# Layer 1 linear attention: quotients in four 32-row strips of the array instead of one 128-row product

## The chip, the cores and the metric

The kernel runs on one core of one Trainium2 chip. The metric is the device time of one execution in microseconds (us), the median over several runs. The engines are named as in the profile: PE is TensorE (PEld its weight loads), DVE is VectorE, ACT is ScalarE, POOL is GpSimd, SP is SyncE. PSUM has eight banks, 0 to 7, of 512 float32 columns.

## The reference, cut to what matters

The whole program is two transformer layers on x[4, 1024, 256]: layer 0 (causal attention plus a mixture of 8 experts, top 2) and layer 1 (linear attention plus an RWKV channel mix). The change is in the attention of layer 1, which has 16 heads of 16 columns:

```python
qkv = (x @ W_qkv).reshape(B, T, 3, H, hd).transpose(2, 0, 3, 1, 4)
q, k, v = (qkv[0], qkv[1], qkv[2])
q = _apply_rope(q, cos, sin)
k = _apply_rope(k, cos, sin)
q_feat = jax.nn.elu(q * SCALE) + 1.0
k_feat = jax.nn.elu(k) + 1.0
kv = jnp.einsum('bhtd,bhtv->bhdv', k_feat, v)
k_sum = k_feat.sum(axis=2)
denom = jnp.maximum(jnp.einsum('bhtd,bhd->bht', q_feat, k_sum), 1e-06)
out = jnp.einsum('bhtd,bhdv->bhtv', q_feat, kv) / denom[..., None]
out = out.transpose(0, 2, 1, 3).reshape(B, T, D)
return out @ W_out
```

Beside it, on the same normed input: `sigmoid(xr @ W_r.T) * (relu(xk @ W_k.T)**2 @ W_v.T)`. Both are added to x.

## The kernel before, in words

`combine_and_layer1` does layer 1 for the four sequences one after the other; `body(b, first, last)` of each engine holds the work of sequence b (0 and 3 written out, 1 and 2 in a loop). There is no scheduler: each engine does its instructions in the order in which they are written, and semaphores join the engines. A sequence is 8 token tiles of 128 tokens, D = 256 columns in DC = 2 chunks `c` of 128, and a chunk holds HP = 8 heads, or NQ = 4 strips of Q = 32 columns with two heads each.

PE's order in a sequence, after the projections q, k, v (L1716 to L1718, from parts), the channel mix's k and r (L1710, L1711) and the transposes of q (L1859):

1. The sums k_feat' v (L1867): per chunk and strip a matmul with 32 columns of weights and 33 moving columns (32 of v and a one, which gives k_sum), into banks 4 and 5. They use four column strips of the array.
2. `mix_values` (L1710, L1711 with act_k): the value product of the channel mix for pairs of token tiles n = 0, 1, 2, in banks 6, 7, 0.
3. `quotients([0, 1])` (L1887): for each token tile i and chunk c one matmul of 128 rows, weights qT (transposed q, kept in xkT, 128 columns), moving `kv` [128, 136]: 128 columns of numerators and 8 of denominators. `kv` is block diagonal over heads, so DVE has masked it (L2274, L2277). One token tile fills one bank, banks 2 to 5 for n = 0, 1.
4. `mix_values([3])` (bank 1), `quotients([2])` (banks 6, 7), `turn_attention(0)` (L1898, transposes of the first four tiles of the result `att` into banks 2, 3), `quotients([3])` (banks 0, 1), `project_out(0)` (L1710, L1711 with wout, banks 4, 5), `turn_attention(1)`, the transposes of the next sequence's first half (L1704), `project_out(1)`, and those of its second half.

All these are float32; the profile has two PE records, each with its weight load, for one such matmul that is not a transpose. So quotients are 16 matmuls and 32 records a sequence.

DVE's order around it: add expert rows for sequence b + 1 (L2103), mask kv (L2274, L2277), more rows (L2103), `scales` (L2134, L2136), `apply_gate(0)` and `(1)` (L2251), `divide(0)` and `(1)`, `apply_gate(2)` and `(3)`, `measure` (L2116, L2120), `divide(2)` and `(3)`, then the sums of the output (L2300). A `divide(n)` serves two token tiles: a maximum (L2258), a reciprocal (L2260) and one multiply per token tile (L2263, [128, 256], from PSUM). A gate reads the bank of a `mix_values` product. ACT copies the transposed q out of banks 0 to 3 (L2065, semaphore qT_ready) and `att` out of banks 2 and 3 (L2074, semaphore oT_ready).

```python
def quotients(pairs):
    for n in pairs:
        if n >= 2:
            pe.wait_ge(gated, NG * b + 2 * (n - 1))
```

Of the kernel before, what the change touches and what calls it, by code (L numbers as in the profile page):

```python
# [1472 lines left out]
def combine_and_layer1(nc, s, expert_out, W_out, mu_r, mu_k, rope_cos, rope_sin, out):  # L1473
# [8 lines left out]
    with ExitStack() as ctx:  # L1482
# [34 lines left out]
        kv = sb("kv", [P, DC, P + HP])  # L1517
        same_head, head_of = sb("same_head", [P, P]), sb("head_of", [P, HP])
# [9 lines left out]
        den = sb("den", [P, 2, 2, DC, HP])  # L1528

# [97 lines left out]
        def _(pool):  # L1627
# [34 lines left out]
            pool.wait_ge(const_ready, 5)  # L1662
            pool.tensor_copy(head_of[:, :], heads[:, :, 0]).then_inc(const_ready, 1)
# [25 lines left out]
        def _(pe):  # L1689
# [126 lines left out]
            def body(b, first, last):  # L1816
# [53 lines left out]
                def mix_values(pairs):  # L1870

                    for n in pairs:
                        if n == 2:
                            pe.wait_ge(qT_ready, 4 * b + 2)
                        for j in range(2):
                            mm = product(ps[:, (6 + n) % 8, j * D:(j + 1) * D],
                                         lambda c: act_k[:, c, tile_of(2 * n + j)], lambda c: wT[:, 2, c, :])
# [3 lines left out]
                def quotients(pairs):  # L1881
                    for n in pairs:
                        if n >= 2:
                            pe.wait_ge(gated, NG * b + 2 * (n - 1))
                        for i in (2 * n, 2 * n + 1):
                            for c in range(DC):
                                mm = pe.matmul(ps[:, (2 + i) % 8, c * (P + HP):(c + 1) * (P + HP)],  # L1887
                                               qT[:, c, tile_of(i)], kv[:, c, :], start=True, stop=True)
                        mm.then_inc(nd_mm, 1)

                def turn_attention(h):
# [4 lines left out]
                    for c in range(DC):  # L1896
                        for i in range(4):
                            mm = pe.transpose(ps[:, 2 + c, tile_of(i)], att[:, 4 * h + i, tile_of(c)], s.ident[:, :])  # L1898
# [16 lines left out]
                quotients([0, 1])  # L1915
                mix_values([3])
                quotients([2])
                turn_attention(0)
                quotients([3])
# [13 lines left out]
        def _(act):  # L1933
# [79 lines left out]
            def body(b, first, last):  # L2013
# [8 lines left out]
                if not first:  # L2022
                    act.wait_ge(nd_mm, NG * b)
# [45 lines left out]
                for m in range(4):  # L2069
# [4 lines left out]
                    act.activation(oT[:, c, h * HB:(h + 1) * HB], ps[:, 2 + c, :], ACT.Copy).then_inc(oT_ready, 1)  # L2074
# [10 lines left out]
        def _(dve):  # L2085
# [117 lines left out]
            def body(b, first, last):  # L2203
# [44 lines left out]
                def apply_gate(n):  # L2248
                    dve.wait_ge(v_mm, NG * b + n + 1)
                    at = gate[:, 2 * n:2 * n + 2, :]  # L2250
                    V.scalar_tensor_tensor(at, at, 1.0, pair_of_tiles(ps[:, (6 + n) % 8, :]), ALU.add, ALU.mult  # L2251
                                           ).then_inc(gated, 1)

                def divide(n):
                    dve.wait_ge(nd_mm, NG * b + n + 1)
                    two = slice((2 + 2 * n) % 8, (2 + 2 * n) % 8 + 2)
# [115 lines left out]
```

## Time and profile before

| | |
|---|---|
| median of 3 runs | 900.39 us (899.24 to 901.1) |
| the profiled execution | 899.21 us |
| its span, first to last instruction | 897.5 us |
| granted TensorE clock, mean | 0.994 of full speed |
| PE busy | 852.9 us, 95% of the span |
| DVE busy | 689.2 us, 77% |
| ACT busy | 523.8 us, 58% |
| POOL busy | 173.2 us, 19% |

Layer 1 is the last quarter of the span; the four places of the change lie near 705 to 717, 761 to 773, 817 to 829 and 873 to 885 us. Matmul records overlap, and a record's length holds its way through the array; the distance from start to start says what one costs PE in a row of them.

### The profile page before, as it was taken

How to read it: one execution, taken by the hardware profiler on the slowest of the kernel's cores; microseconds unless marked ns; L12 is line 12 of the kernel's file. 1: busy time of each engine (PE TensorE's matmuls, PEld its weight loads, DVE VectorE, ACT ScalarE, POOL GpSimd, SP SyncE). 2: the span in 40 equal slices, each digit the busy share in tenths (PEclk: the TensorE clock that was granted, in tenths of full speed). 3: DMA queues.
4: the chain of work that ended last, by engine and by line, in shares of the span. 5: the costliest groups of instructions: out<-in, count | busy, mean ns of one | idle time of the engine just before them, and what ended most of it. 6: DMA issues, size and time to landing. Idle time of an engine off the chain costs nothing. (4 is left out here: it accounts for less than half of the span.)

```text
span 897.5 us, 16848 instructions
## 1 busy us (share of the span) xinstructions
PE 852.9 (95%) x6067; PEld 762.8 (85%) x6067; DVE 689.2 (77%) x1306; ACT 523.8 (58%) x946; POOL 173.2 (19%) x187
## 2 busy tenths in 40 slices
PE   4998989989999999999999999999899999999998
PEld 3787979879999999998989899998787887879877
DVE  6788675566688887888787878785579989899864
ACT  5634354355647565746465665646288678586781
POOL 1000000130120213021111112003506246252202
PEclk9999999999999999999999999999999999999999
DMA  8302000073457575665748383842202122031101
GB/s 288 124 2 95 1 1 1 25 241 121 139 188 259 189 249 184 225 218 196 246 164 279 124 280 128 276 158 60 71 1 65 31 71 72 1 105 35 47 1 48
DMA packets 77396, 112.42 MB, mean 125 GB/s; under 512 B 7552, under 2 KB 64192, under 8 KB 77344
## 3 DMA queue, kind: packets, MB, share of 16 engines
q1 hardware_dynamic: 70864, 94.03, 31.0%
q0 software_dynamic: 6480, 17.70, 6.7%
q8 instruction: 31, 0.51, 0.2%
q14 instruction: 21, 0.17, 0.1%
HBM read 94.02 MB, written 17.69 MB: 124 GB/s over the span
## 5 line engine op out<-in xcount | busy, mean ns | idle before, releaser
L1336 ACT ACTIVATE h<-ps,b1T 128x512 f32<-128x512 f32 (+1 forms) x160 | 90.4, 588 | 126.6 <-PE ps L1200 125.2
L1198 PE MATMUL ps<-w2h,hh 128*128 128x256 f32 x568 | 162.8, 287 | 0.0
L1200 PE MATMUL ps<-w2h,hl 128*128 128x256 f32 x568 | 160.7, 283 | 0.0
L1199 PE MATMUL ps<-w2l,hh 128*128 128x256 f32 x568 | 160.6, 283 | 0.0
L117 POOL DMA_INDIRECT rows<-xn_rows,row_tokens x49 | 49.4, 1007 | 471.1 <-PE ps L1206 310.8
L1441 DVE TENSOR_TENSOR hl<-h,hh 128x512 fp32r<-128x512 f32 x124 | 85.6, 690 | 70.9 <-ACT hh L1340 62.4
L1198 PE MATMUL ps<-xTh,w1h 128*128 128x512 f32 (+1 forms) x320 | 110.6, 345 | 2.4 <-DVE xTl L1383 2.4
L1198 PEld LDWEIGHTS ps<-w2h,hh 128*128 128x128 f32 x568 | 108.6, 191 | 2.4 <-DVE hl L1441 0.2
L1199 PE MATMUL ps<-xTl,w1h 128*128 128x512 f32 (+1 forms) x320 | 110.6, 346 | 0.0
L1199 PEld LDWEIGHTS ps<-w2l,hh 128*128 128x128 f32 x568 | 108.7, 191 | 2.1
L1200 PE MATMUL ps<-xTh,w1l 128*128 128x512 f32 (+1 forms) x320 | 110.0, 344 | 0.0
L1200 PEld LDWEIGHTS ps<-w2h,hl 128*128 128x128 f32 x568 | 108.6, 191 | 0.0
L1340 ACT ACTIVATE hh<-h 128x512 fp32r<-128x512 f32 x124 | 78.4, 633 | 3.9
L127 POOL DMA_INDIRECT raw<-expert_out,slots x48 | 57.8, 1205 | 61.9 <-PE ps L1718 49.5
L1198 PEld LDWEIGHTS ps<-xTh,w1h 128*128 128x128 f32 x320 | 61.4, 192 | 8.0 <-DVE xTl L1383 2.6
L1200 PEld LDWEIGHTS ps<-xTh,w1l 128*128 128x128 f32 x320 | 61.1, 191 | 7.4
L1199 PEld LDWEIGHTS ps<-xTl,w1h 128*128 128x128 f32 x320 | 61.2, 191 | 5.0
L1716 PE MATMUL ps<-wqkvh,xh 128*128 128x256 f32 (+1 forms) x128 | 43.6, 341 | 2.4 <-DVE folded L2093 2.4
L1717 PE MATMUL ps<-wqkvl,xh 128*128 128x256 f32 (+1 forms) x128 | 43.3, 338 | 0.0
L1377 DVE TENSOR_TENSOR w2l<-raw,w2h 128x512 fp32r<-128x512 f32 x60 | 41.6, 694 | 2.1
L1718 PE MATMUL ps<-wqkvh,folded 128*128 128x256 f32 (+1 forms) x128 | 43.1, 337 | 0.0
L611 ACT ACTIVATE shared<-ps,neg_max 128x1024 f32<-128x1024 f32 (+7 forms) x24 | 17.6, 737 | 42.6 <-DVE neg_max L916 42.6
(327 smaller groups left out, 2173.4 us busy)
## 6 DMA issues: line engine op xcount, KB each, us to landing
raw<-in_L_ffn_W SPq DMA_DIRECT2D x30, 1024.0 KB, 5.0
raw_odd<-in_L_ffn_W SPq DMA_DIRECT2D x28, 1024.0 KB
expert_out<-y SPq DMA_DIRECT2D x11, 512.0 KB
shared<-in_L_ffn_b SPq DMA_DIRECT2D x9, 512.0 KB
b2row<-in_L_ffn_b SPq DMA_DIRECT2D x29, 128.0 KB, 8.7
x_acc<-in_L_attn_x SPq DMA_DIRECT2D x3, 1024.0 KB, 8.8
xn_rows<-raw SPq DMA_DIRECT2D x3, 1024.0 KB, 4.4
out<-x_acc SPq DMA_DIRECT2D x3, 1024.0 KB
```

Of the source, the lines that this page charges most:

```text
L117: pool.indirect_dma_start(out=rows_part(s, tile, part), out_offset=None, in_=xn_rows, in_offset=bass.IndirectOffsetOnAxis(ap=token, axis=0 ...
L127: pool.indirect_dma_start(out=s.picked_rows[:, i, k, :], out_offset=None, in_=expert_out, in_offset=bass.IndirectOffsetOnAxis(ap=slot, axi ...
L1198: pe.matmul(out, ah, bh, start=start, stop=False, skip_group_check=True)
L1199: pe.matmul(out, ah, bl, start=False, stop=False, skip_group_check=True)
L1200: return pe.matmul(out, al, bh, start=False, stop=stop, skip_group_check=True)
L1336: op = act.activation(h32[:, at, cols], ps[:, slot, cols], ACT.Relu, bias=s.b1T[:, ds(e * HC + w * tile.chunks + n, 1)])
L1340: act.activation(hh[:, slot, 0:tile.width], h32[:, at, 0:tile.width], ACT.Copy).then_inc(h_hi, 1)
L1377: V.tensor_tensor(w2l[:, u, ks], w2raw[u][:, ks], w2h[:, u, ks].bitcast(F32), ALU.subtract).then_inc(w2_lo, 1)
L1441: V.tensor_tensor(hl[:, slot, at], h32[:, slot % 2, at], hh[:, slot, at].bitcast(F32), ALU.subtract).then_inc(h_lo, 1)
L1716: pe.matmul(dst, ah(c), bh(c), start=(c == 0), stop=False)
L1717: pe.matmul(dst, ah(c), bl(c), start=False, stop=False)
L1718: mm = pe.matmul(dst, al(c), bh(c), start=False, stop=(c == DC - 1))
```

## The change

The quotients are computed per strip: for each token tile, chunk and strip q of 32 rows, one matmul whose weights are 32 rows and 128 columns of qT and whose moving tensor is 34 columns of `kv` (32 numerators, 2 denominators). `kv` becomes [128, 2, 34]; the mask is 32 columns wide (`same_in_strip`, reduced once from `same_head` on DVE before the sequences; a POOL copy falls away). Strip q writes to bank 4 + q for token tiles 0 to 3 and to bank q for tiles 4 to 7. So there are 64 matmuls a sequence instead of 16, in two calls of 32, each with one semaphore increment at its end; `divide` reads four banks and multiplies in four instructions instead of two. The value products move to banks 0 to 3, and each waits for ACT's copy of the transposed q out of that bank. `turn_attention(0)` writes to banks 6 and 7. Before the second call PE waits for all four gates.

```diff
@@ -1514,8 +1514,9 @@
         Q, NQ = 32, P // 32
         v1 = sb("v1", [P, BT, DC, NQ, Q + 1])
         qT = xkT
-        kv = sb("kv", [P, DC, P + HP])
-        same_head, head_of = sb("same_head", [P, P]), sb("head_of", [P, HP])
+        HQ = Q // HD
+        kv = sb("kv", [P, DC, Q + HQ])
+        same_head, same_in_strip = sb("same_head", [P, P]), sb("same_in_strip", [P, Q])
...
+        def quotient_columns(i, c, q):
+
+            at = ((i % 4) * DC + c) * (Q + HQ)
+            return ps[:, 4 * (1 - i // 4) + q, at:at + Q + HQ]
+
+        def quotients_of(n):
+
+            first = 4 * (1 - n // 2)
+            at = n % 2 * 2 * DC * (Q + HQ)
+            return ps[:, first:first + NQ, at:at + 2 * DC * (Q + HQ)].rearrange("p q (m f) -> p m q f", f=Q + HQ)
+
+        def turned_bank(h, c):
+
+            return (6 if h == 0 else 2) + c
...
                     for n in pairs:
-                        if n == 2:
-                            pe.wait_ge(qT_ready, 4 * b + 2)
+                        pe.wait_ge(qT_ready, 4 * b + n + 1)
                         for j in range(2):
-                            mm = product(ps[:, (6 + n) % 8, j * D:(j + 1) * D],
+                            mm = product(ps[:, n, j * D:(j + 1) * D],
                                          lambda c: act_k[:, c, tile_of(2 * n + j)], lambda c: wT[:, 2, c, :])
                         mm.then_inc(v_mm, 1)
...
-                def quotients(pairs):
-                    for n in pairs:
-                        if n >= 2:
-                            pe.wait_ge(gated, NG * b + 2 * (n - 1))
-                        for i in (2 * n, 2 * n + 1):
-                            for c in range(DC):
-                                mm = pe.matmul(ps[:, (2 + i) % 8, c * (P + HP):(c + 1) * (P + HP)],
-                                               qT[:, c, tile_of(i)], kv[:, c, :], start=True, stop=True)
-                        mm.then_inc(nd_mm, 1)
+                def quotients(half):
+                    if half:
+                        pe.wait_ge(gated, NG * b + NG)
+                    for i in range(4 * half, 4 * half + 4):
+                        for c in range(DC):
+                            for q in range(NQ):
+                                of = slice(q * Q, (q + 1) * Q)
+                                mm = pe.matmul(quotient_columns(i, c, q), qT[of, c, tile_of(i)], kv[of, c, :],
+                                               start=True, stop=True)
+                    mm.then_inc(nd_mm, 1)
...
-                            mm = pe.transpose(ps[:, 2 + c, tile_of(i)], att[:, 4 * h + i, tile_of(c)], s.ident[:, :])
+                            mm = pe.transpose(ps[:, turned_bank(h, c), tile_of(i)], att[:, 4 * h + i, tile_of(c)],
+                                              s.ident[:, :])
...
-                quotients([0, 1])
+                quotients(0)
                 mix_values([3])
-                quotients([2])
                 turn_attention(0)
-                quotients([3])
+                quotients(1)
                 project_out(0)
...
                 def divide(n):
-                    dve.wait_ge(nd_mm, NG * b + n + 1)
-                    two = slice((2 + 2 * n) % 8, (2 + 2 * n) % 8 + 2)
-                    nd = ps[:, two, 0:DC * (P + HP)].rearrange("p j (c f) -> p j c f", c=DC)
-                    V.tensor_scalar(den[:, n % 2], nd[:, :, :, P:P + HP], 1e-6, None, ALU.max).then_inc(den_step, 1)
+                    dve.wait_ge(nd_mm, 2 * b + n // 2 + 1)
+                    nd = quotients_of(n)
+                    V.tensor_scalar(den[:, n % 2].rearrange("p j c (q h) -> p (j c) q h", h=HQ), nd[:, :, :, Q:Q + HQ], 1e-6, None,
+                                    ALU.max).then_inc(den_step, 1)
...
                     for j in range(2):
-                        op = V.tensor_tensor(att[:, 2 * n + j, :].rearrange("p (c h f) -> p c h f", c=DC, f=HD),
-                                             nd[:, j, :, 0:P].rearrange("p c (h f) -> p c h f", f=HD),
-                                             den[:, n % 2, j].unsqueeze(3).to_broadcast([P, DC, HP, HD]), ALU.mult)
+                        for c in range(DC):
+                            at = slice(c * P, (c + 1) * P)
+                            op = V.tensor_tensor(att[:, 2 * n + j, at].rearrange("p (q h f) -> p q h f", q=NQ, f=HD),
+                                                 nd[:, j * DC + c, :, 0:Q].rearrange("p q (h f) -> p q h f", f=HD),
+                                                 den[:, n % 2, j, c].rearrange("p (q h) -> p q h", h=HQ).unsqueeze(3)
+                                                 .to_broadcast([P, NQ, HQ, HD]), ALU.mult)
                     op.then_inc(att_ready, 1)
...
-                for c in range(DC):
-                    V.tensor_tensor(kv[:, c, 0:P].rearrange("p (q f) -> p q f", f=Q),
-                                    ps[:, 4 + c, 0:Q].unsqueeze(1).to_broadcast([P, NQ, Q]),
-                                    same_head[:, :].rearrange("p (q f) -> p q f", f=Q), ALU.mult)
-                    op = V.tensor_scalar(kv[:, c, P:P + HP], head_of[:, :], ps[:, 4 + c, Q:Q + 1], None, ALU.mult)
-                op.then_inc(kv_ready, 1)
+                V.tensor_tensor(kv[:, :, 0:Q], ps[:, 4:4 + DC, 0:Q],
+                                same_in_strip[:, :].unsqueeze(1).to_broadcast([P, DC, Q]), ALU.mult)
+                V.tensor_tensor(kv[:, :, Q:], ps[:, 4:4 + DC, Q:Q + 1].to_broadcast([P, DC, HQ]),
+                                same_in_strip[:, 0:Q:HD].unsqueeze(1).to_broadcast([P, DC, HQ]), ALU.mult
+                                ).then_inc(kv_ready, 1)
```

PE, the loop body of sequences 1 and 2, from the third value product on (`wT,act_k` is `mix_values`, `kv,xkT` the quotients, `ident,att` the transposes of the result, `wout,oT` the output product). Before:

```order
L1710 MATMUL ps<-wT,act_k 128x256 [waits qT_ready]
L1711 MATMUL ps<-wT,act_k 128x256
L1710 MATMUL ps<-wT,act_k 128x256
L1711 MATMUL ps<-wT,act_k 128x256
L1887 MATMUL ps<-kv,xkT 128x136 [waits kv_ready,qT_ready]
L1887 MATMUL ps<-kv,xkT 128x136 x7
L1710 MATMUL ps<-wT,act_k 128x256
L1711 MATMUL ps<-wT,act_k 128x256
L1710 MATMUL ps<-wT,act_k 128x256
L1711 MATMUL ps<-wT,act_k 128x256
L1887 MATMUL ps<-kv,xkT 128x136 [waits gated]
L1887 MATMUL ps<-kv,xkT 128x136 x3
```

Behind these rows stand, before the change, `turn_attention(0)` (8 transposes, waits att_ready), then 4 more quotients (wait gated), then the output product. Now:

```order
L1901 MATMUL ps<-kv,xkT 128x34 [waits kv_ready,qT_ready]
L1901 MATMUL ps<-kv,xkT 128x34 x31
L1724 MATMUL ps<-wT,act_k 128x256 [waits qT_ready]
L1725 MATMUL ps<-wT,act_k 128x256
L1724 MATMUL ps<-wT,act_k 128x256
L1725 MATMUL ps<-wT,act_k 128x256
L1912 MATMUL ps<-ident,att 128x128 [waits att_ready]
L1912 MATMUL ps<-ident,att 128x128 x7
L1901 MATMUL ps<-kv,xkT 128x34 [waits gated]
L1901 MATMUL ps<-kv,xkT 128x34 x31
L1724 MATMUL ps<-wout,oT 128x256 [waits oT_ready]
L1725 MATMUL ps<-wout,oT 128x256
```

Four of the eight quotient token tiles stood before the first divide could be waited for, and two of the rest before `turn_attention(0)`; now four stand before it and four behind it.

DVE, sequence 0, from the mask of kv to the second pair of gates. Before:

```order
L2274 TENSOR_TENSOR kv<-ps,same_head 128x128 [waits kv_mm,first_added]
L2277 TENSOR_SCALAR kv<-head_of,ps 128x8
L2274 TENSOR_TENSOR kv<-ps,same_head 128x128
L2277 TENSOR_SCALAR kv<-head_of,ps 128x8
L2103 SCALAR_TENSOR_TENSOR x_acc<-raw,gates,x_acc 128x256 x4
L2134 RECIPROCAL rstd<-std 128x4 [waits std_done1]
L2136 SCALAR_TENSOR_TENSOR shift<-mv,rstd 128x4 [waits rstd_done1]
L2251 SCALAR_TENSOR_TENSOR gate<-gate,ps 128x512 [waits v_mm] x2
L2258 TENSOR_SCALAR den<-ps 128x32 [waits nd_mm]
L2260 RECIPROCAL den<-den 128x32 [waits den_step]
L2263 TENSOR_TENSOR att<-ps,den 128x256 [waits den_step]
L2263 TENSOR_TENSOR att<-ps,den 128x256
```

Now:

```order
L2290 TENSOR_TENSOR kv<-ps,same_in_strip 128x2x32 [waits kv_mm,first_added]
L2292 TENSOR_TENSOR kv<-ps,same_in_strip 128x2x2
L2117 SCALAR_TENSOR_TENSOR x_acc<-raw,gates,x_acc 128x256 x4
L2148 RECIPROCAL rstd<-std 128x4 [waits std_done1]
L2150 SCALAR_TENSOR_TENSOR shift<-mv,rstd 128x4 [waits rstd_done1]
L2265 SCALAR_TENSOR_TENSOR gate<-gate,ps 128x512 [waits v_mm] x2
L2271 TENSOR_SCALAR den<-ps 128x32 [waits nd_mm]
L2274 RECIPROCAL den<-den 128x32 [waits den_step]
L2279 TENSOR_TENSOR att<-ps,den 128x128 [waits den_step]
L2279 TENSOR_TENSOR att<-ps,den 128x128 x3
```

The order on DVE stays: gates 0 and 1, divides 0 and 1, gates 2 and 3. Two instructions leave the mask of kv and two come into each divide.

## Rows read from the trace of the kernel before

**Rows 1.** The page: busy time of PE and its neighbours over the span.

```profile
PE 852.9 (95%) x6067; PEld 762.8 (85%) x6067; DVE 689.2 (77%) x1306; ACT 523.8 (58%) x946; POOL 173.2 (19%) x187
```

**Rows 2.** Chain of waits, 766 to 774 us (sequence 1): start, length, what.

```profile
by line: PE ps L1887 46.4%; PE ps L1710 25.2%; PE ps L1711 21.6%; PE ps L1898 10.9%
...
766.74 1.85 PE ps L1887 x16
```

**Rows 3.** Timeline of PE, 766 to 773.2 us: start, length of all, engine, line.

```profile
766.57 2.02 PE L1887 MATMUL ps<-kv,xkT 128*128 128x136 f32 x16
768.43 0.59 PE L1710 MATMUL ps<-wT,act_k 128*128 128x256 f32 x2
...
770.15 1.09 PE L1887 MATMUL ps<-kv,xkT 128*128 128x136 f32 x8
771.08 1.04 PE L1898 MATMUL ps<-ident,att 128*128 128x128 f32 x8
771.95 1.09 PE L1887 MATMUL ps<-kv,xkT 128*128 128x136 f32 x8
772.88 0.67 PE L1710 MATMUL ps<-wout,oT 128*128 128x256 f32 x2
```

**Rows 4.** Timeline of DVE, 764 to 774 us (sequence 1).

```profile
767.70 0.19 DVE L2258 TENSOR_SCALAR den<-ps 128x32 f32<-128x32 f32 x1 [0.26 <-PE ps L1887]
...
768.31 0.76 DVE L2263 TENSOR_TENSOR att<-ps,den 128x256 f32<-128x256 f32 x2
768.99 0.18 DVE L2258 TENSOR_SCALAR den<-ps 128x32 f32<-128x32 f32 x1
...
770.26 1.28 DVE L2251 SCALAR_TENSOR_TENSOR gate<-gate,ps 128x512 f32<-128x512 f32 x2
```

**Rows 5.** The same view of DVE, the mask of kv.

```profile
763.83 0.23 DVE L2277 TENSOR_SCALAR kv<-head_of,ps 128x8 f32<-128x8 f32 x1
763.96 0.28 DVE L2274 TENSOR_TENSOR kv<-ps,same_head 128x128 f32<-128x128 f32 x1
764.16 0.23 DVE L2277 TENSOR_SCALAR kv<-head_of,ps 128x8 f32<-128x8 f32 x1
```

**Rows 6.** Lines L1887 (quotients) and L1867 (sums): ns min/median/max, first and last start.

```profile
L1887 PEld LDWEIGHTS ps<-kv,xkT x128: 190/190/192, 710.0 to 884.9; 128*128 128x128 f32 x128
L1887 PE MATMUL ps<-kv,xkT x128: 279/279/282, 710.2 to 885.0; 128*128 128x136 f32 x128
L1867 PEld LDWEIGHTS ps<-v,feat x512: 106/109/113, 702.9 to 873.4; 128*32 128x32 f32 x171
L1867 PE MATMUL ps<-v,feat x512: 190/197/218, 702.9 to 873.4; 128*32 128x33 f32 x171
```

**Rows 7.** Chain of waits, 600 to 898 us: the sums of sequence 2 and what follows.

```profile
816.23 1.23 PE ps L1867 x118
817.47 0.63 PE ps L1710 x2
818.09 0.43 PE ps L1711 x2
```

**Rows 8.** Timelines of four places: ACT's copies of transposed q and PE's first value product.

```profile
704.74 2.10 ACT L2065 ACTIVATE xkT<-ps 128x512 f32<-128x512 f32 x4
704.95 0.70 PE L1710 MATMUL ps<-wT,act_k 128*128 128x256 f32 x2 [0.75 <-ACT act_k L2048]
...
760.63 2.04 ACT L2065 ACTIVATE xkT<-ps 128x512 f32<-128x512 f32 x4
761.29 0.70 PE L1710 MATMUL ps<-wT,act_k 128*128 128x256 f32 x2
...
817.10 2.04 ACT L2065 ACTIVATE xkT<-ps 128x512 f32<-128x512 f32 x4
817.39 0.70 PE L1710 MATMUL ps<-wT,act_k 128*128 128x256 f32 x2
...
873.27 2.04 ACT L2065 ACTIVATE xkT<-ps 128x512 f32<-128x512 f32 x4
873.56 0.70 PE L1710 MATMUL ps<-wT,act_k 128*128 128x256 f32 x2
```

**Rows 9.** Timeline, 760 to 784 us: ACT's copies of the first half of att.

```profile
771.72 1.08 ACT L2074 ACTIVATE oT<-ps 128x512 f32<-128x512 f32 x2 [3.26 <-PE ps L1898]
```

More of the change, by code:

```diff
@@ L1661, in _ @@
                                pattern=[[HD, HP], [0, HD]], channel_multiplier=-1).then_inc(const_ready, 1)
-            pool.wait_ge(const_ready, 5)
-            pool.tensor_copy(head_of[:, :], heads[:, :, 0]).then_inc(const_ready, 1)
             for i in range(1, BT):
@@ L2022, in body @@
                 if not first:
-                    act.wait_ge(nd_mm, NG * b)
+                    act.wait_ge(nd_mm, 2 * b)
                 scaled(b)
@@ L2073, in body @@
                     act.wait_ge(att_turned, 4 * b + m + 1)
-                    act.activation(oT[:, c, h * HB:(h + 1) * HB], ps[:, 2 + c, :], ACT.Copy).then_inc(oT_ready, 1)
+                    act.activation(oT[:, c, h * HB:(h + 1) * HB], ps[:, turned_bank(h, c), :], ACT.Copy).then_inc(oT_ready, 1)
                     if m == 3 and not last:
@@ L2250, in apply_gate @@
                     at = gate[:, 2 * n:2 * n + 2, :]
-                    V.scalar_tensor_tensor(at, at, 1.0, pair_of_tiles(ps[:, (6 + n) % 8, :]), ALU.add, ALU.mult
+                    V.scalar_tensor_tensor(at, at, 1.0, pair_of_tiles(ps[:, n, :]), ALU.add, ALU.mult
                                            ).then_inc(gated, 1)
                 def divide(n):
-                    dve.wait_ge(nd_mm, NG * b + n + 1)
-                    two = slice((2 + 2 * n) % 8, (2 + 2 * n) % 8 + 2)
-                    nd = ps[:, two, 0:DC * (P + HP)].rearrange("p j (c f) -> p j c f", c=DC)
-                    V.tensor_scalar(den[:, n % 2], nd[:, :, :, P:P + HP], 1e-6, None, ALU.max).then_inc(den_step, 1)
+                    dve.wait_ge(nd_mm, 2 * b + n // 2 + 1)
+                    nd = quotients_of(n)
+                    V.tensor_scalar(den[:, n % 2].rearrange("p j c (q h) -> p (j c) q h", h=HQ), nd[:, :, :, Q:Q + HQ], 1e-6, None,
+                                    ALU.max).then_inc(den_step, 1)
                     dve.wait_ge(den_step, 2 * (NG * b + n) + 1)
@@ L2307, in _ @@
             dve.wait_ge(mu_ready, 1)
+            dve.wait_ge(const_ready, 5)
+            V.tensor_reduce(same_in_strip[:, :], same_head[:, :].rearrange("p (q f) -> p f q", f=Q), X, ALU.add
+                            ).then_inc(const_ready, 1)
             dve.wait_ge(const_ready, 6)
```

## The prediction

> **What bounds the kernel now.** I read the page first. PE is busy 95% of the span and DVE 77% [rows 1], so whatever the change does to PE's own work or makes PE wait for counts nearly in full. Then the chain of waits at one of the four places of the change: in sequence 1 it is PE all through, and the quotients hold 46% of those 8 us [rows 2]. The timeline of PE gives the stretch that I compare: from the first quotient (766.57) to the first output product (772.88) 6.31 us pass, without a stall in it [rows 3]. It holds 16 + 8 + 8 quotient records, 8 of the value product and 8 transposes. Last, DVE in the same stretch: it waits 0.26 us for the first quotients, then works without a pause to the end of the second pair of gates, at 770.26 + 1.28 = 771.54 [rows 4]. PE needs a part of that for its next quotients. So PE sets the time and DVE is close behind; the two are a loop, PE to DVE to PE, inside the stretch.
>
> **What a quotient costs.** Now 16 records take 1.85 us [rows 2], 116 ns each: 136 moving columns. So 32 records are 3.7 us a sequence. After, there are 64 matmuls and, with two records each, 128 records of 34 columns. If only the moving columns counted and the four strips ran side by side, one would cost 116 x 34/136 / 4 = 7.2 ns. But each record loads its own weights, and these keep their 128 columns. The loads' lengths are 190 ns for 128 columns and 106 to 109 for 32 [rows 6]: 96 columns are 81 to 84 ns, 0.87 a column, so 128 columns hold a strip's load path about 111 ns (an estimate from these two rows; 116 ns per pair of load and matmul is its ceiling in the trace). Four strips side by side then give 111/4 = 28 ns a record, one after the other 111. The lower end is 7.2. That strips can run side by side at all shows in the sums: 118 records, in four column strips, take 1.23 us [rows 7], 10.4 ns each, while one's load alone is 106 ns long. No row shows strips of rows. I take **28 ns**: the load has 128 columns as in L1887, the overlap is that of L1867. Then 64 records are 1.79 us and both halves 3.58: PE's quotient work does not shrink, though the moving columns fell by four.
>
> The Trainium skill ("TensorE: Matmul & The Clock Gate", LDWEIGHTS (loading the stationary operand)) says that a load's time goes by its columns, not its rows, and that 32 rows take as long as 128. By its figure, columns/1.2 in ns, the 128 columns are 107 ns; the sum would be 0.7 us lower over the four sequences. The rows here agree on the columns; none has fewer than 128 rows, so it is this rule that speaks against the change, and the trace can't yet. The same page ("Wait — 56ns, not 53.3ns?") puts a floor of 25 ns under the distance of two matmuls; the sums' 10.4 ns [rows 7] stand against it, so I do not use it.
>
> **Changing the shape of the array.** Where the sums end and 128 x 128 weights begin, two records take 0.63 us instead of 0.43 [rows 7]: 0.20 to leave strips. To enter them PE starts with a load that nothing covers: 0.19 at most for 128 columns [rows 6], 0 at least; I take 0.15 for the first half and 0.19 for the second, before which PE stands idle. The sequence has two such visits more.
>
> **The loop PE, DVE, PE.** I follow one sequence from the start of the first half, S.
> - First half: 0.15 to enter, 63 x 28 ns to the last record's start, 0.20 for its length [rows 6] and 0.04 to DVE: 2.15. Before, DVE could start at S + 1.13 (767.70), because pair 0 had its own increment; now the increment comes after all four token tiles. DVE's gates 0 and 1 are over by then.
> - Two divides. Before, their start to start is 767.70, 768.99, 770.26: 1.28 each [rows 4]. Two multiplies of 256 columns take 768.99 - 768.31 = 0.68 of it. Now four of 128 columns: at the mask of kv such a multiply is followed after 764.16 - 763.96 = 0.20 [rows 5], so 0.82 and +0.14 a divide. Between 0 (reading four banks in strips of 32 costs nothing and the start-up hides) and +0.44 (four at the 0.28 that one lasts [rows 5]) I take 0.14: two are 2.84.
> - Two gates 1.28 [rows 4], 0.05 to PE: 1.33. PE waits for the last, since the second half overwrites all four banks of the value products. Meanwhile it has the value product (1.72) and `turn_attention(0)` (0.87), which waits for the divides until S + 5.0 and ends at S + 5.9; the gates are done at S + 6.3. So this work is hidden, and gone as cover: PE idles about 1.1 us ahead of the transposes and 0.4 behind them.
> - Second half: 0.19 to enter, 1.79, 0.20 to leave: 2.18.
>
> 2.15 + 2.84 + 1.33 + 2.18 = 8.50 us against 6.31: **+2.2 us a sequence**, 8.8 for four. The output product's other condition, ACT's copies of att, keeps its distance: before, it began 1.80 after the transposes (771.08 to 772.88) and 0.03 after the copies [rows 3, 9]; S + 5.0 + 1.8 is less than 8.5. Divides 2 and 3 take 2.84 under the output product's first half, 3.44 (16 records of 0.43/2 [rows 7]): hidden, by about half a microsecond. What follows is moved as it stands.
>
> **The value products' new wait.** Each now waits for ACT's copy out of its bank. ACT's four take 2.04 to 2.10, so the first is over 0.52 after its start; PE's first value product begins 0.21, 0.66, 0.29 and 0.29 after that start in sequences 0 to 3 [rows 8]. That is late by 0.31, 0 and twice 0.23, and 0.04 for the semaphore each: 0.9 us together. The later three have 1.7 us more per product and don't wait. At the other end it is 0, if the wait lies in the pipeline; it can't be over 1.3.
>
> **Small ones.** The mask of kv falls from four instructions to two, about 0.4 us of DVE a sequence. It ends gates 0 and 1 earlier, at about S + 0.4, and DVE then waits for the first half anyway: nothing. The one reduce before the sequences and the POOL copy are single instructions in front of waits for ACT: nothing. The 96 more records a sequence of matmuls and as many loads have to be fetched; the sums' 128 run at 10.4 ns, so nothing.
>
> **Sum**: 8.8 + 0.9 = 9.7 us on the profiled execution's 899.2 gives 908.9. The median of the runs is 1.2 above that execution, so I give 910.1 for the median.
>
> **Rivals.**
> 1. *Strips as short as the sums'*: the loads of the strips hide each other fully, 10.4 ns a record. For: the sums do it, with 32 columns. Against: 128 columns of weights. A half falls from 1.79 to 0.67, and the loop is 8.50 - 2 x 1.12 = 6.3: no gain, since DVE's divides and gates stand between the halves whatever PE does. With the 0.9 it gives 901.1. Chance 0.10.
> 2. *Faster*: the moving columns alone decide, 7.2 ns, and the four-bank multiplies cost no more than the two did. The halves are 0.46 each, the divides 2.56: 8.50 - 2 x 1.33 - 0.28 = 5.56, -0.75 a sequence. With 0.9 that is -2.1: 898.3. It decides from about 8 ns a record, which no load of 128 columns in the trace comes near. Chance 0.05.
> 3. *Two strips at a time*: the two records of one matmul use the same strip, so only neighbours overlap. 56 ns a record adds 64 x 28 ns to each half, 3.6 a sequence: 924.4. For: the program's order, pass after pass in one strip; against: the sums have the same order and overlap more. Chance 0.12.
> 4. *One at a time*: the loads of row strips share one path. 111 ns a record, +5.3 a half: 952.6. For: no row shows row strips; the column strips of the sums write to different partitions and may have paths that row strips lack. The skill ("TensorEngine Tiling (Array Packing)", Key Properties) lets different tiles load and multiply in parallel, against this one. Chance 0.11.
> 5. *The change doesn't do what it says*: strips are run as full-height products. That would be rival 4's time; it is in its chance.
>
> **How the numbers follow.** My forecast has 0.62. Its own bounds: 0 to 0.44 a divide, 0 to 0.19 an entry, 27 to 29 ns: 1.7 to 3.0 a sequence, 907 to 914. The range has to hold 8 in 10: it takes in rival 1 (most of it) and rival 3, and leaves rivals 2 and 4 out: 900 to 925.5. A measurement of this kernel can tell 0.2%, 1.8 us, from no change. Faster by more is rival 2, 0.05; within it rival 1, 0.10; slower the rest, 0.85.
>
> **What would show it.** Quotient records about 28 ns apart, 64 in 1.8 us, loads 190 ns long. DVE's first maximum of a sequence waits for PE over 1 us instead of 0.26. PE idle before `turn_attention(0)`, released by a DVE multiply, and before the second half, released by a gate. The stretch from first quotient to first output product 8.5 us. The first value product waits for ACT in sequences 0, 2 and 3. The forecast is wrong if the distance is near 10 ns (then the stretch is 6.3), or near 56 or 111; or if it is 28 and the divides are much longer than 1.42.

## The result, and the profile after

The changed kernel takes 911.87 us in the median of 4 runs (910.21 to 920.66), the kernel before 900.51 beside it (899.24 to 901.1): ratio 1.0152, 95% interval 1.012 to 1.0185. The medians are 11.4 us apart. The profiled execution took 911.72 us; its span is 910.0, 12.5 more than before.

The page of the changed kernel, busy times, against [rows 1]:

```profile
PE 858.1 (94%) x6451; PEld 763.9 (84%) x6451; DVE 689.6 (76%) x1331; ACT 523.5 (58%) x946; POOL 174.7 (19%) x186
```

PE has 384 more records and is busy 5.2 us longer; the other engines' totals stand still. The remaining 7.3 of the added 12.5 us are idle time of PE, and the page does not say where. It is found in the stretch from first quotient to first output product. Timeline of PE, 772 to 781.6 us (sequence 1), the answer to [rows 3]:

```profile
772.69 1.99 PE L1901 MATMUL ps<-kv,xkT 32*128 32x34 f32 x64
774.61 0.70 PE L1724 MATMUL ps<-wT,act_k 128*128 128x256 f32 x2
...
776.01 0.59 PE L1725 MATMUL ps<-wT,act_k 128*128 128x256 f32 x2
777.70 1.09 PE L1912 MATMUL ps<-ident,att 128*128 128x128 f32 x8 [1.10 <-DVE att L2279]
778.89 1.99 PE L1901 MATMUL ps<-kv,xkT 32*128 32x34 f32 x64
780.81 0.70 PE L1724 MATMUL ps<-wout,oT 128*128 128x256 f32 x2
```

From 772.69 to 780.81 are 8.12 us, 6.31 before. PE idles 1.10 us ahead of the transposes, until DVE's multiply, and a little ahead of the second half. Each half takes as long as 16 full-height records did: 1.92 us from its first record to the next operation's, against 1.86 in [rows 3].

Timeline of DVE in the same stretch, the answer to [rows 4]:

```profile
774.74 0.19 DVE L2271 TENSOR_SCALAR den<-ps 128x32 f32<-128x32 f32 x1 [1.68 <-PE ps L1901]
...
775.36 0.88 DVE L2279 TENSOR_TENSOR att<-ps,den 128x128 f32<-128x128 f32 x4
776.16 0.18 DVE L2271 TENSOR_SCALAR den<-ps 128x32 f32<-128x32 f32 x1
...
776.76 0.88 DVE L2279 TENSOR_TENSOR att<-ps,den 128x128 f32<-128x128 f32 x4
777.56 1.27 DVE L2265 SCALAR_TENSOR_TENSOR gate<-gate,ps 128x512 f32<-128x512 f32 x2
```

DVE waits 1.68 us for the first half, where it waited 0.26. It then works without a pause until 777.56 + 1.27 = 778.83, and PE starts its second half 0.06 us later. The chain of waits from 772 to 781 us says the same, against [rows 2], where PE held all of it:

```profile
by line: PE ps L1901 43.9%; DVE att L2279 16.2%; DVE gate L2265 13.4%; PE ps L1724 9.4%; DVE den L2274 8.1%; issue 5.2%; PE ps L1725 4.8%; DVE den L2271 3.5%
...
772.76 1.96 PE ps L1901 x64
...
777.64 1.20 DVE gate L2265 x2
778.85 0.04 issue
778.89 1.99 PE ps L1901 x64
```

The chain leaves PE at 774.72 and comes back at 778.89: two divides and two gates of DVE are now on the path. The quotients themselves, by line, against [rows 6]:

```profile
L1901 PEld LDWEIGHTS ps<-kv,xkT x512: 181/187/333, 712.8 to 897.4; 32*128 32x128 f32 x171
L1901 PE MATMUL ps<-kv,xkT x512: 272/273/399, 712.8 to 897.5; 32*128 32x34 f32 x171
```

A load of 32 rows and 128 columns is 187 ns long, one of 128 rows was 190. 64 records in 1.72 us from the first start to the last are 27.3 ns each. The starts of single records, in the same trace, come in rounds of four, by all appearance one in each strip: 7, 6 and 7 ns apart, and then the next round begins 111 or 112 ns after this one (132 behind the first round). So inside a half a record costs 28.0 ns, and a round takes as long as the prediction estimated for one load of 128 columns, 111.

**Account.** From the first sum of sequence 0 to the end the profile has 10.6 us more than before. It divides so, by the starts of the same operations in both traces: the four stretches +2.00, +1.81, +1.81 and +1.80; the first value product later against the sums by 0.59, 0.07, 0.43 and 0.43; the first quotient later against it by 0.06 to 0.07 each; and in sequence 0 the output product lasts 10.12 instead of 8.65 us, +1.47. The other 1.9 of the 12.5 lie ahead of layer 1, in which the two kernels do the same but for one reduce of the mask in place of a POOL copy; over the first 100 us the granted clock was 1.00 before and 0.95 here. Three profiled executions of the changed kernel (`a_again` and `a_third` below are the others) begin their first sum at 704.81, 701.08 and 704.74 us and all take 205.2 us from there to the end, so the part ahead of it varies by itself. Before, the first sum to the end took 194.6. That 1.47 is the clock's. Windows of the changed kernel, around the end of the stretch in sequence 0 (the columns are: window, length, busy time and count of PE, PEld, DVE, ACT, POOL, granted clock, DMA share, GB/s):

```profile
717.00:719.00 2.00, 1.10 (x10) 0.87 (x10) 2.00 (x7) 0.51 (x2) 0.00 (x0) 1.00 0.00 0
719.00:720.00 1.00, 1.00 (x36) 1.00 (x38) 1.00 (x4) 0.58 (x2) 0.00 (x0) 1.00 0.00 0
720.00:721.00 1.00, 1.00 (x36) 1.00 (x32) 0.63 (x5) 0.18 (x1) 0.00 (x0) 0.82 0.06 16
721.00:722.00 1.00, 1.00 (x6) 0.84 (x6) 0.71 (x3) 0.12 (x1) 0.00 (x0) 0.50 0.00 0
...
724.00:725.00 1.00, 1.00 (x6) 0.90 (x5) 0.78 (x4) 0.00 (x0) 0.00 (x0) 0.97 0.00 0
```

The granted clock is 1.00 (2.4 GHz), then 0.50 (1.2 GHz) for some three and a half microseconds, then 1.00 again. Before it fell PE had idled 0.9 us of 2, run the transposes, then most of the 64 strip records. Timeline of PE there:

```profile
721.10 1.22 PE L1724 MATMUL ps<-wout,oT 128*128 128x256 f32 x2
722.12 1.06 PE L1725 MATMUL ps<-wout,oT 128*128 128x256 f32 x2
```

The pairs of the output product that last 0.70 and 0.59 us in sequence 1 last 1.22 and 1.06 here.

### The profile page after: what moved, and what is told of

Read it like the earlier page. It is cut to its first block and busy times, and to the rows that moved or that the text cites. A ratio compares the mean times of both kernels' runs of the same rounds, so it can differ in the third digit from the quotient of the medians.

```text
span 910.0 us, 17645 instructions
## 1 busy us (share of the span) xinstructions
PE 858.1 (94%) x6451; PEld 763.9 (84%) x6451; DVE 689.6 (76%) x1331; ACT 523.5 (58%) x946; POOL 174.7 (19%) x186
```

## The experiments

The theory: strips are bound by their loads at some 28 ns a record, so PE has the same work, and the time goes where the increment and the gates' wait, now one for four token tiles instead of two, make PE and DVE take turns. The rivals: the strips themselves cost the time; the divides over four banks do; the waits do not matter and the clock does. Three chips served, and the kernel before took 900.61 (10 runs), 896.49 (7) and 895.9 us (17) on them; each ratio is against the kernel before on the same chip. "The stretch" is always the one from first quotient to first output product.

**e1_grouped.** The kernel before, with the change's grouping and nothing of its strips.

```diff
-                        if n >= 2:
-                            pe.wait_ge(gated, NG * b + 2 * (n - 1))
+                        if n == 2:
+                            pe.wait_ge(gated, NG * b + NG)
...
-                        mm.then_inc(nd_mm, 1)
+                    mm.then_inc(nd_mm, 1)
...
-                quotients([2])
                 turn_attention(0)
-                quotients([3])
+                quotients([2, 3])
...
-                    dve.wait_ge(nd_mm, NG * b + n + 1)
+                    dve.wait_ge(nd_mm, 2 * b + n // 2 + 1)
```

> The kernel before, 128-row quotients, with the change's grouping alone: one increment after token tiles 0 to 3, all four gates before tiles 4 to 7. Theory (the loop PE, DVE, PE is the cost, the strips are not): first quotient to first output product 1.74 + 0.32 + 2.56 + 1.33 + 1.86 = 7.8 us instead of 6.31, so +1.5 us a sequence, +6 us in all, about 906.5. Rival (the strips and the four-bank divides are the cost): the stretch stays within 0.3 us of 6.31 and the time within 1.5 us of the kernel before.

Measured: 906.4 us (903.73 to 908.19), ratio 1.0052 (1.0034 to 1.007). Timeline of its PE, sequence 1:

```profile
769.74 2.02 PE L1887 MATMUL ps<-kv,xkT 128*128 128x136 f32 x16
...
774.49 1.09 PE L1898 MATMUL ps<-ident,att 128*128 128x128 f32 x8 [1.01 <-DVE att L2262]
775.68 2.12 PE L1887 MATMUL ps<-kv,xkT 128*128 128x136 f32 x16
777.64 0.59 PE L1710 MATMUL ps<-wout,oT 128*128 128x256 f32 x2
```

and of its DVE:

```profile
771.79 0.19 DVE L2257 TENSOR_SCALAR den<-ps 128x32 f32<-128x32 f32 x1 [1.11 <-PE ps L1887]
...
774.35 1.28 DVE L2250 SCALAR_TENSOR_TENSOR gate<-gate,ps 128x512 f32<-128x512 f32 x2
```

The stretch is 7.90 us. Of the 1.81 that the change adds to it, 1.59 come with the grouping alone, without a single strip; what is left for strips and four-bank divides is 0.22. The two traces split it: two divides take 2.82 us in the changed kernel (774.74 to 777.56) and 2.56 here (771.79 to 774.35), +0.26, and the second half 1.92 against 1.96, -0.04. DVE starts 2.05 us after the first quotient in both. So the strips themselves cost nothing, and the divides over four banks a quarter of a microsecond. This is the run that decides.

The edit does more than merge the increments: it also puts the quotients of token tiles 4 and 5 behind the transposes and the gates. By the traces DVE starts 0.92 us later (2.05 after the first quotient, 1.13 before), 16 records instead of 8 stand behind the gates (1.96 us instead of 0.93: +1.03), and the 0.36 that PE's last quotients had to spare behind the gates is used up: 0.92 + 1.03 - 0.36 = 1.59. No run makes only one of the two moves.

**e2_gate2_first.** The changed kernel with gate 2 ahead of the divides, so that the second half should wait for one gate less.

```diff
                 apply_gate(1)
+                apply_gate(2)
                 divide(0)
                 divide(1)
-                apply_gate(2)
                 apply_gate(3)
```

> The changed kernel with gate 2 ahead of divides 0 and 1, where DVE waits over 1 us for the first half. Theory (DVE's queue between the halves sets the second half): the second half starts 0.64 us earlier, the stretch falls from 8.12 to 7.5 us, 2.6 us less than the changed kernel in all, about 909. Rival (PE's own work sets it): nothing moves.

Measured: 911.58 (909.18 to 911.74), ratio 1.0112 (1.0089 to 1.0135); the stretch 7.96 in sequence 1, so only 0.16 of the hoped 0.64 came. Timeline of its PE, sequence 1:

```profile
778.24 1.09 PE L1912 MATMUL ps<-ident,att 128*128 128x128 f32 x8 [1.10 <-DVE att L2279]
779.26 1.99 PE L1901 MATMUL ps<-kv,xkT 32*128 32x34 f32 x64
```

A miss: the second half starts 1.02 after the start of the transposes, directly behind them. I had counted the wait for the gates and forgotten what stands ahead of it in PE's program: with the gate's 0.64 gone, the transposes, which wait for the divides, hold the second half instead.

**e3_double_moving.** 68 moving columns in place of 34; the second 34 are overwritten by the next record, and zeros behind the last.

```diff
...
-            return ps[:, 4 * (1 - i // 4) + q, at:at + Q + HQ]
+            return ps[:, 4 * (1 - i // 4) + q, at:at + 2 * (Q + HQ)]
...
-        mm = pe.matmul(quotient_columns(i, c, q), qT[of, c, tile_of(i)], kv[of, c, :],
+        mm = pe.matmul(quotient_columns(i, c, q), qT[of, c, tile_of(i)], kv[of, c:c + 2, :].rearrange("p c f -> p (c f)"),
...
```

> The changed kernel with 68 moving columns instead of 34 in each quotient matmul; the extra 34 are overwritten by the next one. Theory (a strip's record lasts as long as its load of 128 columns): 64 records still in 1.72 us, 27 ns each, stretch unchanged at 8.1. Rival (moving columns or the writes to PSUM set it): 54 ns or more each, halves near 3.5 us, stretch 8.1 + 3.5 = 11.6.

Measured: 910.5 (1 run). Its timeline and its line of loads:

```profile
771.30 2.02 PE L1901 MATMUL ps<-kv,xkT 32*128 32x68 f32 x64
```

```profile
L1901 PEld LDWEIGHTS ps<-kv,xkT x512: 181/187/187, 713.0 to 896.2; 32*128 32x128 f32 x171
```

Twice the moving columns, and 64 records take 1.75 us instead of 1.72, 27.7 ns each; the rounds of four are again 111 to 112 ns apart, and only the first is longer (163 ns for 132). So moving columns, and with them the columns written to PSUM, are nearly free here, as a bound by the loads wants.

**e4_same_strip.** The changed kernel with the strip in the outermost loop: the same records, neighbours in the same strip.

```diff
-                    for i in range(4 * half, 4 * half + 4):
-                        for c in range(DC):
-                            for q in range(NQ):
+                    for q in range(NQ):
+                        for i in range(4 * half, 4 * half + 4):
+                            for c in range(DC):
```

> The changed kernel with the loop over strips outermost, so that eight matmuls in a row use the same strip. Theory (loads overlap only between different strips that stand next to each other): 109 ns a record, each half 7.0 us instead of 1.72, stretch 8.1 + 10.5 = 18.7 us, about +42 us in all. Rival (PE looks far enough ahead to fill the other strips, or the 27 ns is a rate of its own that owes nothing to strips): 27 ns a record, no change.

Measured: 971.21 (1 run). Timeline of its PE:

```profile
784.46 7.98 PE L1901 MATMUL ps<-kv,xkT 32*128 32x34 f32 x64
792.37 1.22 PE L1724 MATMUL ps<-wT,act_k 128*128 128x256 f32 x2
```

A half takes 7.4 to 9.0 us from its first record's start to its last one's, 117 to 143 ns a record, but this mean mixes two clocks: in every one of the eight halves a part runs at half clock. Windows of the first half of sequence 0 (columns as above):

```profile
711.00:713.00 2.00, 2.00 (x28) 2.00 (x28) 0.00 (x0) 0.00 (x0) 0.00 (x0) 1.00 0.00 0
713.00:714.00 1.00, 1.00 (x9) 1.00 (x7) 0.00 (x0) 0.00 (x0) 0.00 (x0) 0.59 0.00 0
717.00:718.00 1.00, 1.00 (x6) 0.93 (x6) 0.00 (x0) 0.00 (x0) 0.00 (x0) 0.50 0.00 0
```

Inside a strip the records start 111 or 112 ns apart at full clock, the 111 estimated for one load, and 213 or 214 at half clock; only where one strip's records meet the next one's are they closer. Four times 28.0 is 112: so the changed kernel's order, strip after strip inside a tile, gives the factor of four, and its records are not "two at a time" nor "one at a time". Over the parts at full clock the mean distance is 89 to 96 ns, the places where strips meet included; at that pace the eight halves would cost some 33 us more than the changed kernel's (an estimate from these distances), less than the 42 expected. The rest of the 59 above its 911.87 goes with the half clock (mean granted clock 0.952).

**e5_half_tiles.** The changed kernel, each quotient product cut in two of 64 weight columns: twice the records, half the load each.

```diff
+        HT = P // 2
...
-        mm = pe.matmul(quotient_columns(i, c, q), qT[of, c, tile_of(i)], kv[of, c, :],
-                       start=True, stop=True)
+        for t in range(2):
+            mm = pe.matmul(quotient_columns(i, c, q)[t * HT:(t + 1) * HT],
+                           qT[of, c, i * P + t * HT:i * P + (t + 1) * HT], kv[of, c, :],
+                           start=True, stop=True)
```

> The changed kernel with each quotient matmul cut in two of 64 weight columns (64 tokens), so eight pieces of the array of 32 rows and 64 columns; 256 records a sequence. Theory (a record lasts as long as its load and the pieces run side by side): 64 columns load in 56 ns, eight side by side give 7 ns a record, so a half of 128 records takes about 0.9 to 1.1 us instead of 1.72 and the stretch falls from 8.12 to about 6.7 us. Rival (pieces that share rows don't load side by side, or a matmul of any size costs some 13 ns or more of issue): a half stays at 1.7 us or grows to 3.4.

Measured: 900.09 (1 run; 3.6 above the median before). Its PE timeline, sequence 1, and its line of loads:

```profile
764.11 1.49 PE L1905 MATMUL ps<-kv,xkT 32*64 32x34 f32 x128
...
768.59 1.09 PE L1917 MATMUL ps<-ident,att 128*128 128x128 f32 x8 [1.07 <-DVE att L2284]
769.78 1.49 PE L1905 MATMUL ps<-kv,xkT 32*64 32x34 f32 x128
771.21 0.70 PE L1727 MATMUL ps<-wout,oT 128*128 128x256 f32 x2
```

```profile
L1905 PEld LDWEIGHTS ps<-kv,xkT x1024: 127/131/133, 706.9 to 885.8; 32*64 32x64 f32 x171
```

The 128 records of a half take 1.27 us, 10.0 ns each, where I expected 7 to 8.5; that is 0.45 us less than the changed kernel's 1.72, though they are twice as many. The stretch is 7.10 (764.11 to 771.21), 1.02 less, where 6.7 was expected; the two halves, each 1.42 us to the next operation instead of 1.92, are all of it. PE's own work does fall in this form, below the 3.7 us of the kernel before, and the kernel is still no faster than the one before, since DVE stands between the halves.

**e6_half_tiles_gate2.** The edits of e5 and e2 together.

> The half-width pieces and gate 2 ahead of divides 0 and 1. If the half takes 1.0 us, DVE starts the divides at S + 1.25, PE transposes at S + 4.1, and the second half starts behind them at S + 5.05: stretch 6.3 to 6.5 us, that of the kernel before (6.31). With the 1.5 us of the value products' waits the time would be about 902 to 903. If PE's work alone set the stretch, it would be 5.2 us and the time 898.

Measured: 902.77 (901.1 to 904.67), ratio 1.0069 (1.0046 to 1.0091), the stretch 6.93 against the expected 6.3 to 6.5. By its own trace it is 0.17 a sequence better than e5; its time is no better than e5's one run. As expected, the second half starts directly behind the transposes. The miss is the length of the halves: 1.27 us from first to last record where 1.0 stood in the sum, so DVE starts its divides 1.53 us after the first quotient, not 1.25, PE its transposes at 4.49, not 4.1, and the second half is longer too.

**e7_early_copy.** The changed kernel with ACT's copy of the first transposed q ahead of two of the four squares (`copy_q(n)` is the old loop's body as a function). PE's first two value products wait for two squares only, the third for all four; that part of the edit is not shown.

```diff
-                for n in range(4):
-                    square(n)
-                for n in range(4):
+                square(0)
+                square(2)
+                copy_q(0)
+                square(1)
+                square(3)
+                for n in range(1, 4):
+                    copy_q(n)
...
```

> The changed kernel with ACT's squares in the order 0, 2, then the first copy of transposed q, then squares 1 and 3; PE's first two value products wait for two squares. Theory (the first value product is late by ACT's first copy): from the first sum to the first value product 1.6 us or less in sequence 0 (2.64 in the changed kernel) and 1.2 us in 2 and 3 (1.66), 1.5 to 2 us less in all. Rival (the delay lies in leaving the strips, not in the copy): unchanged.

Measured: 904.99 (1 run). From the first sum to the first value product 1.61, 1.23, 1.23 and 1.23 us in the four sequences, against 2.64, 1.67, 1.66 and 1.66 in the changed kernel. Sequence 0 of the changed kernel:

```profile
704.81 1.30 PE L1881 MATMUL ps<-v,feat 128*32 128x33 f32 x128
...
707.45 0.67 PE L1724 MATMUL ps<-wT,act_k 128*128 128x256 f32 x2 [1.34 <-ACT xkT L2079]
```

and of e7:

```profile
701.95 1.30 PE L1881 MATMUL ps<-v,feat 128*32 128x33 f32 x128
703.55 0.67 PE L1724 MATMUL ps<-wT,act_k 128*128 128x256 f32 x2 [0.31 <-ACT xkT L2079]
```

The wait is the one predicted, for ACT's copy, and it goes when the copy comes early: in sequences 2 and 3 the first value product is back at the 1.23 us of the kernel before. Sequence 0 gains 1.03, more than the 0.59 that the change had cost it, because the edit also shortens the wait for the squares, which the kernel before had (2.05 there).

**a_again.** The changed kernel once more, on e5 to e7's chip.

> The changed kernel once more, unchanged, for its spread and for the granted clock. If the half clock between 719 and 724.5 us in sequence 0 comes from the change (strips of 34 columns after 1.3 us of idle PE), it stands in this profile too, at the second half of a sequence; if it was chance, it is gone, and the stretch from first to last output product of sequence 0 is 8.65 us instead of 10.1.

Measured: 911.53 (904.49 to 915.14), ratio 1.0163 (1.01 to 1.0225). The half clock came back, in another sequence. Windows of its stretch in sequence 1:

```profile
773.00:775.00 2.00, 1.90 (x57) 1.66 (x55) 1.85 (x6) 1.08 (x2) 0.00 (x0) 1.00 0.03 8
775.00:777.00 2.00, 2.00 (x24) 1.67 (x21) 1.64 (x10) 0.30 (x1) 0.00 (x0) 0.59 0.00 0
777.00:779.00 2.00, 2.00 (x7) 1.61 (x6) 1.72 (x9) 0.00 (x0) 0.00 (x0) 0.56 0.00 0
779.00:781.00 2.00, 2.00 (x13) 1.74 (x12) 0.69 (x1) 0.00 (x0) 0.95 (x1) 1.00 0.00 0
```

In this execution sequence 0 ran at full clock and sequence 1 did not. Its time from the first sum to the end is nevertheless the same, 205.2 us in both.

**e8_all_strips.** The edits of e5, e2 and e7 together: the best version with strips that I could make.

> The three mends together on the changed kernel: pieces of 64 tokens, gate 2 ahead of the divides, ACT's first copy between the squares. Theory (what is left is DVE's divides behind the first half and the change of shape): stretch 6.9 us against 6.31, 2.5 us in all, less 0.8 us for a first value product that starts earlier than in the kernel before in sequences 0 and 1: 1.7 us over the kernel before. Rival (strips could still win once PE is free): at or under the kernel before.

Measured: 900.3 (899.97 to 900.64), ratio 1.0057 (1.0041 to 1.0072). From the first sum to the end its profile has 2.9 us more than before, where 1.7 was expected: the stretch is 6.93 at best, 7.69 in sequence 0. In sequence 0 the last two of the 128 records of the first half come some 0.7 us late, for no reason that the profile shows. The version takes back more than half of the change's loss and still does not reach the kernel before.

**e9_before_early.** The edit of e7 made to the kernel before.

> The kernel before with only ACT's order (squares 0, 2, copy, squares 1, 3) and two squares waited for: the first value product starts 0.4 us earlier in sequence 0 and 0.4 in sequence 1, not in 2 and 3; the stretch stays 6.31 us; 0.8 us (0.1%) less in all, too little to be told from no change by time.

Measured: 896.64 (894.71 to 901.42, 12 runs), ratio 1.0009 (0.9995 to 1.0023): no difference. Its first value product comes 1.23 us after the first sum in all four sequences, 0.8 us earlier in sequence 0, and there the stretch grows from 6.31 to 6.91. What ACT gives, DVE takes: PE's transposes then wait for a divide and its last eight quotient records for the gates, 0.06 us behind each.

**e3_double_again and a_third.** e3 and the changed kernel side by side on e8's chip, to see whether the half clock hangs on the small strips.

> 68 moving columns, timed this time, for the granted clock. If the drop to half clock at a second half comes from strips that do little per record, 68 columns make it rarer: the runs lie closer together than those of the changed kernel and their median is 1 to 3 us lower, though PE streams twice the columns. If it is chance or comes from the idle stretch before, the two are alike.

> The changed kernel beside the one with 68 moving columns on the same chip: spread over the runs 5 us or more if the drops are its own, and a drop to half clock at a second half in the profile, as twice before; within 3 us and none if they were chance.

Measured: 906.82 (904.5 to 908.02), ratio 1.0126 (1.0107 to 1.0146), and 906.56 (903.37 to 911.67), ratio 1.0122 (1.0102 to 1.0142). The profile with 68 columns again has no half clock at the quotients; that of the changed kernel has a spell, in sequence 3, where the output product lasts 10.17 us. The medians are the same, where 1 to 3 us less was expected with 68 columns if the small strips bring the spells; the spread is 3.5 us (4 runs) for the one and 8.3 (5 runs) for the other.

## Why the prediction was right

The direction, the size and the mechanism came out: 910.1 forecast, 911.87 measured. That the two lie so close is in part luck: the terms of the sum are 0.7 us too high together, and two things that it does not have, the spell of half clock and 1.9 us ahead of layer 1, make up for more. By steps:

- **A record of the strips: 28 ns forecast, 28.0 in the rounds of four, 27.3 as the mean of a half** (its last round has only its starts in the sum). Its two assumptions hold apart: the load goes by its 128 columns (187 ns long with 32 rows, 190 with 128; a round is 112 ns against the forecast 111), and four strips overlap fully (e4: 112 ns a record, at full clock, once they don't). e3 shows that the moving columns don't decide. The Trainium skill ("TensorE: Matmul & The Clock Gate", LDWEIGHTS (loading the stationary operand)) had said that rows don't matter, with 107 ns for these columns; this case's trace now agrees on the rows and has 112 ns. The floor of 25 ns between matmuls, which the Trainium skill gives in "TensorE: Matmul & The Clock Gate" ("Wait — 56ns, not 53.3ns?"), would explain 27.3 as well; the 7 ns between the starts inside a round, and e5 with 10.0 ns a record, rule it out as the bound here.
- **Rivals 1 and 2** (strips as short as the sums', moving columns alone) fall with 27.3 ns; **rivals 3 and 4** too, at 56 and 111 ns. e4 is rival 4 brought about: 971 us, more than its 952.6; the 112 ns a record are rival 4's 111, and what is above goes with the half clock.
- **DVE's start**: S + 2.15 forecast, 772.69 to 774.74 = 2.05 measured. **A divide**: 1.42 forecast, 774.74 to 776.16 = 1.42 measured. **Transposes** at S + 5.0, measured 5.01. **Second half** after the gates: they end at S + 6.14 (forecast 6.3).
- **Entering the array's strips**: 0.15 and 0.19 forecast. Ahead of the first half it is 0.10: from the last pair of value product records to the first strip record 0.53 us (772.16 to 772.69), 0.43 before, and it lies ahead of the stretch, not in it. The account's 0.06 to 0.07 is this less 0.03, which the first value product gives back. The second costs nothing to be seen, because PE is idle ahead of it: its first record starts 0.06 after the gate's end, semaphore included, as the 128-row record of e1 does. Where the half follows the transposes directly (e2), 0.20 us pass from the last transpose's start to the first strip record, and 0.11 before the change: 0.09 again. Leaving them costs the 0.20 (a half is 1.72 and another 0.20 from its last record to the next product). So the loop is 8.12 instead of 8.50: **+1.8 a sequence, not +2.2**.
- **The value products' new wait**: 0.9 forecast, 0.59 + 0.07 + 0.43 + 0.43 = 1.5 measured. This is the mis-sized term, and 1.5 lies above the 1.3 that the prediction called its limit. I had put the first copy's end a quarter of four copies after its start, 0.52, and 0.04 for the semaphore. The copies overlap: in the changed kernel, sequence 0, the second starts 0.48 after the first, but the first holds PE from its start at 706.66 until 707.31, 0.65. Then 0.14 pass until the product, where before, behind ACT's square, it was 0.05. The trace has PE's own semaphore instruction in between (707.34 to 707.39), then the load (707.42), then the product. ACT's copies and the chain of waits:

```profile
706.66 2.10 ACT L2079 ACTIVATE xkT<-ps 128x512 f32<-128x512 f32 x4
```

```profile
706.82 0.50 ACT xkT L2079
707.31 0.14 issue
707.45 0.67 PE ps L1724 x2
```

- **Sum**: stretches 4 x 1.81, entries 0.26, waits 1.5, together 9.0 us, for 9.7. Two errors of opposite sign cancel in part.
- **Not in the prediction**: the spell at 1.2 GHz, 1.66 us in the profiled execution (1.47 in the output product and 0.19 in the stretch), and the 1.9 us ahead of layer 1. Their first sums start at 704.59, 705.48 and 704.87 us in e1 to e3, as late as the changed kernel's 704.81 (702.90 before), and in e1 with not one strip; so they are no matter of the strips. With both, 9.0 becomes the 12.5 of the trace.

Runs of equal mean clock bear the 9.0 out: a_again's one run at 0.994 took 904.49, 8.4 and 9.8 above the two runs before at 0.994 on that chip (896.1 and 894.65); a_third's two (903.37 and 906.43) average 904.9, 9.3 above the three before at 0.994 there (895.9, 894.23 and 896.74, mean 895.6).

What stays open is what lowers the clock. Apart from e4, the four profiles with spells at this place (the changed kernel's three and e2's) have 34 moving columns and an idle stretch ahead of the transposes; e7 has both and no spell (nor have e5, e6 and e8, with their shorter loads); e3, twice with 68 columns and the same idle, has none; nor has e1 with the idle and no strips. In e4's sequence 0 the clock falls at 713.2 us, in the middle of same-strip records and with no idle PE since 704.4, so strip records can do it without an idle stretch. That points to the sparse strips, but the median with 68 columns equals a_third's, so it is not shown for the changed kernel.

## What to carry to other kernels

Cost a matmul with few rows by its weight columns: here, cutting the rows of the array in four left each load as long as before, four of them overlapped, and nothing was won; only shorter weights (e5) made the records faster, and they overlap only where neighbours are in different strips (e4). Before the tiles of a group share one signal, walk once round the loop of both engines: here the work on either engine hardly changed, and 1.6 of 1.8 us a sequence came from the grouping, one signal per four tiles instead of two and twice the quotients behind the gates. And after taking a wait away, ask what stands ahead of it in the same engine's program (e2).

## What the runs showed that I had not expected

- 32 x 64 pieces: 10.0 ns a record, though a load is 131 ns long; 32 x 128: 27.3 ns with 187. Half the weight columns gave 0.37 of the distance, not half. The forecast's way of counting puts 64 columns at 0.87 x 64 = 56 ns (an estimate), so 10.0 lies between four (14) and eight (7) of them side by side. In the trace eight records in a row take 58 ns at best, which is eight side by side, but up to 150 at other places of a half, the same ones in every half. Why these lag is not settled.
- Neighbours in one strip cost 112 ns a record at full clock, four times the 28.0 in different strips, and they bring the half clock with them: the order of the loops alone is worth some 59 us of this kernel (971.21, one run, against 911.87).
- Spells at 1.2 GHz of some 3.5 us, at the end of a stretch of strip records or right behind it, in the changed kernel in a different sequence from execution to execution, about 1.5 us each.
